# A decoder layer on one core: another written order of the steps of its four chunks

## The reference

```
x = layernorm(x + self_attention(x))              # 16 heads of 8, scores also get q . rel_k[distance],
                                                  # values also get weights . rel_v[distance]
x = layernorm(x + cross_attention(x, ctx))        # 16 heads of 8, causal
x = layernorm(x + shared(x) + sum of 8 experts)   # each 128 -> 256 -> gelu -> 128, weighted by
                                                  # the router's softmax, cut to its top 2
```

## Time and profile before

| | us |
|---|---|
| median of three timed executions | 483.2 |
| lowest and highest | 480.25, 483.86 |
| the profiled execution | 484.97 |
| its span in the profile | 482.9 |
| mean granted clock of TensorE in it | 0.929 |

### The profile page before, as it was taken

How to read it: one execution, slowest core, us unless ns; L and a number is a source line. 1 busy time by engine, 2 the same in 40 slices (tenths; PEclk the granted TensorE clock), 3 DMA queues, 4 the chain that set the end, 5 groups by cost and what they waited for, 6 DMA issues and landing times.

```text
span 482.9 us, 11287 instructions
## 1 busy us (share of the span) xinstructions
PE 406.3 (84%) x4718; PEld 302.9 (63%) x4729; DVE 324.4 (67%) x630; ACT 248.0 (51%) x329; POOL 76.4 (16%) x84
## 2 busy tenths in 40 slices
...
DMA packets 29324, 26.87 MB, mean 56 GB/s; under 512 B 12577, under 2 KB 27866, under 8 KB 28506
## 3 DMA queue, kind: packets, MB, share of 16 engines
...
...
## 4 chain that ended last, share of the span: by engine, by line
PE 55%; DVE 22%; ACT 8%; DMA 5%; issue 4%; SPq 4%; POOL 1%; POOLq 0%; DVEq 0%; ACTq 0%
PE ps_f L708 12%; PE ps_f L719 11%; PE ps_s L545 8%; PE ps_f L571 5%; PE ps_f L671 3%; DVE ST L930 3%; DVE ST L960 3%; DMA QS<-MP 3%; PE ps_f L579 2%; ACT ST L786 2%; DVE MX L933 2%; PE ps_s L538 2%; PE ps_f L518 2%; PE ps_f L524 2%; SPq L414 2%
## 5 line engine op out<-in xcount | busy, mean ns | idle before, releaser
L545 PE MATMUL ps_s<-QS,KS 125*128 125x128 bf16 (+1 forms) x768 | 80.6, 249 | 16.7 <-DVE ST L930 11.2
L545 PEld LDWEIGHTS ps_s<-QS,KS 125*128 125x128 bf16 (+1 forms) x768 | 64.4, 106 | 43.9 <-issue 14.9
L833 ACT ACTIVATE HT<-ps_f,hb 128x512 f32<-128x512 f32 x72 | 48.9, 689 | 81.5 <-PE ps_f L708 39.2
L719 PEld LDWEIGHTS ps_f<-w,HT 128*128 128x128 f32 x576 | 69.2, 192 | 10.0 <-issue 7.4
L708 PE MATMUL ps_f<-x2T,w 128*128 128x512 f32 x144 | 73.5, 619 | 0.0
L719 PE MATMUL ps_f<-w,HT 128*128 128x128 f32 x576 | 73.3, 278 | 0.0
L790 ACT ACTIVATE ST<-ST 128x1024 f32<-128x1024 f32 x32 | 33.6, 1060 | 52.1 <-DVE ST L960 51.7
L1044 DVE SCALAR_TENSOR_TENSOR acc<-ps_f,gw,acc 128x128 f32<-128x128 f32 x128 | 37.4, 363 | 31.3 <-PE ps_f L719 31.2
L483 POOL TENSOR_SCALAR_AFFINE_SELECT PC<-PC 128x1024 f32<-128x1024 f32 x32 | 34.8, 1096 | 147.8 <-ACT PC L797 147.7
L930 DVE TENSOR_TENSOR ST<-ps_s,ST 128x1024 f32<-128x1024 f32 x32 | 38.6, 1207 | 13.4 <-PE ps_s L545 13.4
L937 DVE TRANSPOSE_TENSOR_REDUCE MX<-ps_s 128x32 f32<-128x1024 f32 x32 | 39.0, 1237 | 7.1 <-PE ps_s L545 7.1
...
## 6 DMA issues: line engine op xcount, KB each, us to landing
...
QS<-MP SPq DMA_DIRECT2D x48, 8.0 KB, 2.1
```

What stands on the lines that cost most here:

```text
L545: last = nc.tensor.matmul(ps[:, o:o + S], KS[a][0:kd, c:c + S], queries(a, kd, h, j), start=not masked and j == 0, stop=j == NB - 1, skip_ ...
L719: last = nc.tensor.matmul(ps[:, b * E:(b + 1) * E], HT[n % 2][:, f, b * S:(b + 1) * S], w2[:, e, f, :], start=f == 0, stop=f == NF - 1 and ...
L833: nc.scalar.activation(HT[n % 2][:, f, :], ps[:, :], ACT.Gelu, bias=hb[:, e, f:f + 1]).then_inc(ht_ready, 1)
```

## The change

SCHEDULE is written in another order; the same steps stand in it, and no other line is changed. The diff, cut to the lines that the text below speaks of:

```diff
-0load 1load 0xT 0q 0v 0k 0cT 0loadc 0st_q 0st_k 1xT 0ck 1q 0bias.0 0cv 0bias.1 0bias.2 0bias.3 0bias.4 0bias.5
-0bias.6 0bias.7 0p1.0 0p1.1 0p1.2 0p1.3 0p1.4 0p1.5 0m.0 0p1.6 0p1.7 0p2.0 0m.1 0p2.1 0p2.2 0p2.3 0pv.0 0p2.4
-0p2.5 0pv.1 0p2.6 0p2.7 0pvT.0 0pvT.1 0pv.2 1st_q 1k 0w2.0 0w2.1 0w2.2 0pv.3 0w2.3 0pvT.2 0pvT.3 0w2T.0 0w2T.1
...
-1bias.7 1p1.0 0x1T 0cq 1p1.1 1p1.2 0st_cq 1cT 1p1.3 1p1.4 2load 1m.0 0c1.0 0c1.1 0c1.2 0c1.3 1p2.0 1p2.1 0c1.4
...
-1p2.6 1p2.7 1cv 2loadc 0cpvT.3 0cX 1pv.2 1ck 1w2.0 0cXT 2k 1w2.1 1pv.3 1w2.2 0co 0cln 1pvT.2 1w2.3 1pvT.3
-2bias.0 1w2T.0 2bias.1 1w2T.1 1w2T.2 1w2T.3 1X 0x2T 2v 0r 1XT 2bias.2 2bias.3 1o 2bias.4 2bias.5 2st_k 0g
...
-0up.17 3loadc 1cm.1 1c2.2 2pv.0 1cpv.0 2p1.6 1c2.3 3xT 2p1.7 2pvT.0 1c2.4 3q 1c2.5 1cpv.1 2m.1 1c2.6 0dn.7
...
-3c1.0 3c1.1 2up.14 3c1.2 3c1.3 2up.15 3c1.4 3cm.0 2up.16 3c1.5 3c1.6 2dn.6 2up.17 3c2.0 3c1.7 2dn.7 3c2.1 3cm.1
-3c2.2 3c2.3 3cpv.0 2dn.8 3c2.4 3c2.5 3cpv.1 3c2.6 3c2.7 3cpv.2 3cpvT.0 2fln 3cX 3cpvT.1 3cpv.3 3cpvT.2 3cpvT.3
...
+0cT 0load 0xT 0loadc 1load 0q 0cv 0st_q 0k 0ck 0v 0bias.0 0bias.1 0bias.2 0bias.3 0bias.4 1loadc 0bias.5 0st_k
+0bias.6 0bias.7 0p1.0 0p1.1 0p1.2 0p1.3 0p1.4 1xT 0p1.5 0m.0 0p1.6 0p1.7 0p2.0 0m.1 0p2.1 0p2.2 0p2.3 0pv.0
+0p2.4 0st_ck 0p2.5 0pv.1 0p2.6 0p2.7 0pvT.0 1q 0pv.2 1k 0w2.0 0w2.1 0w2.2 0pv.3 0pvT.1 0w2.3 0pvT.2 0pvT.3
...
+1v 1p1.0 1st_k 0x1T 0cq 0st_cq 1p1.1 1p1.2 1cT 1p1.3 1m.0 0c1.0 0c1.1 0c1.2 0c1.3 2load 1p2.0 0cm.0 0c1.4 1p2.1
+1p2.2 0c1.5 1p2.3 0c1.6 0c1.7 2xT 1p1.4 1pv.0 0c2.0 0c2.1 0cm.1 0c2.2 1p1.5 1pvT.0 0c2.3 0cpv.0 1p1.6 1pv.1
...
+1p2.7 1cv 0cpvT.3 0cX 1pv.2 2q 1ck 1w2.0 1w2.1 0cXT 1w2.2 1pv.3 2st_q 0co 1pvT.2 1pvT.3 1w2.3 0cln 2bias.0
+1w2T.0 1w2T.1 1w2T.2 1w2T.3 1X 2bias.1 0x2T 2v 1XT 0r 2bias.2 2bias.3 0up.0 1o 2loadc 2bias.4 1ln 1st_ck 2bias.5
+0g 2st_k 2bias.6 2bias.7 3load 0up.1 2p1.0 1x1T 0up.2 1cq 0up.3 0dn.0 2p1.1 3loadc 0up.4 2cT 2p1.2 2p1.3 0up.5
...
+2up.14 3c1.4 3c1.5 3cm.0 2up.15 3c1.6 3c1.7 2dn.6 2up.16 2up.17 3cm.1 3c2.0 3c2.1 2dn.7 2dn.8 3c2.2 3c2.3 3cpv.0
+3c2.4 3c2.5 3cpvT.0 3cpv.1 3c2.6 3c2.7 3cpv.2 3cpvT.1 3cpv.3 3cpvT.2 2fln 3cX 3cpvT.3 3cXT 3co 3cln 3x2T 3r
...
```

More of the change, by code:

```diff
@@ L72 @@
 SCHEDULE = """
-0load 1load 0xT 0q 0v 0k 0cT 0loadc 0st_q 0st_k 1xT 0ck 1q 0bias.0 0cv 0bias.1 0bias.2 0bias.3 0bias.4 0bias.5
-0bias.6 0bias.7 0p1.0 0p1.1 0p1.2 0p1.3 0p1.4 0p1.5 0m.0 0p1.6 0p1.7 0p2.0 0m.1 0p2.1 0p2.2 0p2.3 0pv.0 0p2.4
-0p2.5 0pv.1 0p2.6 0p2.7 0pvT.0 0pvT.1 0pv.2 1st_q 1k 0w2.0 0w2.1 0w2.2 0pv.3 0w2.3 0pvT.2 0pvT.3 0w2T.0 0w2T.1
-0w2T.2 0w2T.3 1bias.0 1loadc 1bias.1 0X 0XT 1bias.2 1bias.3 0o 1bias.4 1bias.5 1v 0ln 0st_ck 1st_k 1bias.6
-1bias.7 1p1.0 0x1T 0cq 1p1.1 1p1.2 0st_cq 1cT 1p1.3 1p1.4 2load 1m.0 0c1.0 0c1.1 0c1.2 0c1.3 1p2.0 1p2.1 0c1.4
@@ L78 @@
-2xT 0cm.0 1pv.0 1p2.2 0c1.5 1p2.3 0c1.6 0c1.7 0c2.0 0cm.1 0c2.1 1p1.5 0c2.2 1pvT.0 1p1.6 0cpv.0 0c2.3 1pv.1
-1p1.7 0cpvT.0 0c2.4 0cpv.1 0c2.5 1m.1 0c2.6 2q 2st_q 0c2.7 0cpv.2 1pvT.1 0cpvT.1 1p2.4 1p2.5 0cpvT.2 0cpv.3
-1p2.6 1p2.7 1cv 2loadc 0cpvT.3 0cX 1pv.2 1ck 1w2.0 0cXT 2k 1w2.1 1pv.3 1w2.2 0co 0cln 1pvT.2 1w2.3 1pvT.3
-2bias.0 1w2T.0 2bias.1 1w2T.1 1w2T.2 1w2T.3 1X 0x2T 2v 0r 1XT 2bias.2 2bias.3 1o 2bias.4 2bias.5 2st_k 0g
-2bias.6 1ln 2bias.7 0up.0 2p1.0 0up.1 1x1T 2p1.1 0up.2 0up.3 1st_ck 3load 1cq 0up.4 0dn.0 2p1.2 0up.5 2p1.3
@@ L83 @@
-0up.6 0dn.1 0up.7 2p1.4 0up.8 1st_cq 0dn.2 0up.9 0up.10 2m.0 1c1.0 0up.11 1c1.1 0dn.3 1c1.2 2p2.0 0dn.4 2cT
-2p2.1 0up.12 1c1.3 0up.13 1c1.4 1cm.0 1c1.5 2ck 1c1.6 0up.14 0dn.5 1c2.0 0dn.6 1c2.1 0up.15 1c1.7 0up.16 2p1.5
-0up.17 3loadc 1cm.1 1c2.2 2pv.0 1cpv.0 2p1.6 1c2.3 3xT 2p1.7 2pvT.0 1c2.4 3q 1c2.5 1cpv.1 2m.1 1c2.6 0dn.7
-1cpvT.0 1c2.7 1cpv.2 2p2.2 1cpvT.1 2p2.3 1cpvT.2 2p2.4 1cpv.3 2p2.5 2cv 2p2.6 2p2.7 0dn.8 1cpvT.3 2pv.1 3st_q
-2pv.2 2w2.0 2pvT.1 2pv.3 1cX 1cXT 0fln 2w2.1 1co 1cln 2w2.2 2pvT.2 2w2.3 2pvT.3 3v 2w2T.0 3k 2w2T.1 3bias.0
@@ L88 @@
[L88 to L92, removed]
```

22 lines of the change are left out of this document (17 added, 5 removed).

## The result

The changed kernel is slower: 497.4 us (median of four, 495.5 to 498.9) against 483.5 (median of four), a ratio of 1.029 with a 95% interval of 1.021 to 1.037. The prediction had 487.8 and a range of 478.5 to 492.5, so it is wrong.

What follows compares the result with a forecast made beforehand. PE was taken as nearly full from 144 to 396 us, DVE as the bound from 36 to 60; 2.1 + 2.1 + 1.7 + 1.5 + 0 - 2.8 = +4.6 on the median 483.2 gave 487.8 us, range 478.5 to 492.5.

Steps and rivals of the forecast that it cites:

- start: First 60 us: the context ahead of x and a later 0st_k delay 0p1.0 by 2.1 us, bounds 1.3 to 3.3.
- 1q beside chunk 0's w2, with 1st_q: Chunk 0's w2: 1q's projection and two slowed splits on ACT cost +2.1 us, from 0.6 to 4.0; 1st_q costs nothing.
- 1p1.4 (and the rest to 1p2.4): Around 0c1: the tile moved behind it costs DVE time on the way to 1p2.4, +1.7 us, from 0 to 2.4.
- 2q beside chunk 1's w2 (1p2.4 to 2bias.0): Chunk 1's w2: 2st_q lands near 165.8 and PE is 1 us later, +1.5 us, from -1 to 3.
- the middle: Chunks 2 and 3 up to 396 us: many small moves, taken as 0, from -3.5 to +2.5 us.
- the tail: Chunk 3's end: no wait at 3c2.4, three 3cpv turns in 10.4 us instead of 13.5; -2.8 us, from -3.5 to -1.
- The wait for the context: Start: PE stands for the context though x is ready; q's low part ends 5.7 us later than before.
- DVE's hole ahead of 0c1.0: Before 0c1.0: DVE is done with 1m.0 at 105.0 and idles for 2 us, as 1p1.4 no longer fills the wait.
- the sign that the prediction named: 165 to 396 us: the prediction is wrong if PE's idle time there changes by more than 3 us.
- the +4.5: Start: if 0st_k's data wait for 640 KB ahead in the ring, it lands near 39.7; +4.5 us, not adopted.
- The step that failed: Chunk 0's w2: 1st_q behind 1k's spread lands about when PE has ended w2T, so it costs nothing: 0 us.
- Rival (d): 0st_k, 1st_q and 2st_q land late, each behind a spread waiting for a split: 493.6, or nearer 491 us; chance 0.17.

Runs made afterwards that it cites:

- e6: The kernel before up to 2bias.0, then the order of the changed kernel: 482.2 us, ratio 0.998 to the kernel before.
- e9: The kernel before with 1q moved directly ahead of 0pv.2 and 1st_q left ahead of 1k: 488.1 us, ratio 1.010.
- e2: The changed kernel with 0cT directly behind 0k and 0cv directly behind 0ck: 491.9 us, ratio 1.019 to the kernel before.
- e4: The changed kernel with 1p1.4 directly ahead of 1m.0, as in the kernel before: 495.0 us, ratio 1.024 to the kernel before.
- e8: The kernel before up to 3c1.0, then the changed kernel's order (new tail alone): 480.9 us against 483.7, ratio 0.9947.
- e7: The kernel before with 1q moved directly ahead of 0pv.2 and 1st_q directly behind 1k: 489.3 us, ratio 1.013.
- e5: The changed kernel with 1pvT.1 and 0cpvT.1 directly ahead of 1p2.4, as in the kernel before: 494.5 us, ratio 1.023.
- e1: The changed kernel with 1st_q directly ahead of 1k and 2st_q directly ahead of 1ck: 491.6 us, ratio 1.017 to the kernel before.
- e10: The changed kernel with the repairs of e1, e2 and e4 together: 484.6 us against 483.7 for the kernel before, ratio 1.0026.
- e11: The kernel before up to 0p1.0, then the changed kernel with the repairs of e1, e4 and e5: 481.9 us against 483.7, ratio 0.9942.

## Why the prediction was wrong, by its steps

| term | predicted | first profile | again |
|---|---|---|---|
| start | +2.1 | +2.6 | +1.8 |
| 1q beside chunk 0's w2, with 1st_q | +2.1 | +5.6 | +4.3 |
| 1bias.0 to 0c1.0 | 0 | +0.4 | -0.3 |
| 1p1.4 (and the rest to 1p2.4) | +1.7 | +1.5 | +1.3 |
| 2q beside chunk 1's w2 (1p2.4 to 2bias.0) | +1.5 | +4.5 | +3.3 |
| the middle | 0 | +1.4 | -0.8 |
| the tail | -2.8 | -2.3 | -2.6 |
| sum, with the end | +4.6 | +13.6 | +6.9 |

The last column is the changed kernel's second profile. The profiled execution of this control was the fastest of its six, and that of the kernel before lay above its median; the medians differ by 12.0 to 13.9. Read 2bias.0 instead: 161.9 to 163.3 in the three runs that keep the old order up to there, 178.0 and 173.8 in the two of the changed one. The reference of the 2q row may be 1 us too long: 1w2.0 to 2bias.0 took 12.8 in the kernel before and 11.8 to 11.9 in the four others with the old order there (e6 to e9).

*Right.* The wait for the context and its size (e2 takes all of it back); that 0p1.0 waits for KS; DVE's hole ahead of 0c1.0 (e4: 1.0 to 1.2 of the 1.7); the middle as no loss (PE idles 3.3 us from 2bias.0 to 3bias.0 before and 3.4 after; the sign that the prediction named, idle time from 165 to 396 changed by more than 3 us, did appear, 7.4 before and 12.3 after, but it comes from the waits up to 2bias.0, which stand after 165 now); the tail, down to the 10.4 us of its three turns (e8 shows it alone). The bound on the start also held: the +4.5 had KS landing near 39.7; PE had it at 37.76, and `0st_k`'s DMAs took 4.3 to 5.8 us, not much over the 4.7 to 5.2 of the earlier trace rows. This does not speak against the rule of the Trainium skill, DMA: Bandwidth & Descriptors, section "Queues, rings and completion order", that a DMA engine takes the descriptors of a ring in order. What failed is the rate that the +4.5 was worked out with, 384 KB in 2.7 us or 142 GB/s: with several DMAs in the queue the profile has 501 GB/s from 32 to 33 us.

*The step that failed.* "`1st_q` on SP now waits behind 1k's spread; it lands at about the time when PE has ended w2T, so it costs nothing." In the first profile it landed 2.9 us after that, and its place costs 3.1 us (e7 against e9). I took PE to reach 1bias.0 late by its own waits and the stack to land about then; but the two delays are one chain: slower splits make the spread of k later, the stack stands behind that, and its third DMA takes 5.5 to 6.4 in the changed order (5.4 before). In all six profiles of this order beside w2 (the changed kernel twice, e2, e4, e5, e7) PE waits 1.95 to 3.43 at 1bias.0; with the stack ahead of k's spread it waits 0.95, 0.1 and 0 (e1, e9, e10). The step even said that nothing covers it any more, and then priced it at zero. Its other half was mis-sized only: the split itself predicted at 2.1 is 3.1 (e9).

*The term that was missing.* The sum counted idle time and gave the clock no price. In the changed kernel's first profile TensorE ran at 1.2 GHz for about 3 us behind 1bias.0, for nearly 7 around 1p2.4 and for 3 to 4 behind 2bias.0. Around 1p2.4 this cost an estimated 1.4 to 1.7 in both profiles (above): most of what separates 3.3 from the 1.5 predicted there, and half of what separates 4.5 from it. The rest is waiting: PE's waits for the two splits (0.79 and 0.62; 1.50 and 0.47 in e1) and the one for `2st_q`, 1.36 to 2.85 in the six profiles that have it behind 1ck's spread and 0 to 0.44 in the three that have it ahead (e1, e10, e11). In time that place is the least certain: 1w2.0 to 2bias.0 took 13.5 to 16.7 in the six, 13.5, 13.2 and 11.7 in the three.

*The rivals.* Rival (d) had this mechanism and a chance of 0.17: stacks that land late because each stands behind a spread that waits for a split, with 491 to 493.6. It was right on `1st_q` and `2st_q` and wrong on `0st_k`, where it put the largest part of its excess, and even it had no price for the clock. The evidence that should have moved weight to it was in the profile: `1st_q` went at 66.89 and had landed some 8 us before 1bias.0 needed it at 81.77 (its third DMA starts 1.2 later and took 5.4), and my own sum left nothing of that. An estimate of no slack deserved a price on both sides, and I gave it one number, zero.

*Open.* Why the clock falls behind the wait of 2.39 in e5 and not behind 3.19 in the kernel before, and behind one of two equal waits of 2.46: no run takes that apart. Nor was 2q's move tried alone, nor the changed order of the stretch from 1p2.4 to 1w2.0 seen at the full clock.
